# Exponentials of two latent attentions in eight pieces per head, with the negated row maximum as bias and the row sum from the accumulator

## Chip, core and metric

The kernel runs on one core of one Trainium2 chip. The metric is device microseconds of one execution of the whole program, lower is better; the number for a kernel is the median of several executions. The program is a decoder of four layers in eleven stages that follow each other; the change touches two of them.

## What is computed

`x` has 16 sequences of 64 tokens with 256 channels. The two sublayers that the change touches are the third layer's latent cross attention and the fourth (last) layer's latent self attention. Both end in the same softmax over 64 keys, for 16 heads:

```python
# third layer, cross (cut)
q_r = jnp.einsum('bshq,hqr->bhsr', rope(q_big), W_qr)
k_r = jnp.einsum('bld,hdr->bhlr', kv_r, W_kr)
scores = jnp.einsum('bhsr,bhlr->bhsl', q_r, k_r)
attn = jax.nn.softmax(scores, axis=-1)
ctx_c = jnp.einsum('bhsl,bld->bhsd', attn, kv_r)
# last layer, self attention (cut)
scores = jnp.einsum('bqhd,bkhd->bhqk', qf, kf) * (1.0 / np.sqrt(192))
scores = jnp.where(mask, scores, min)      # causal
p = jax.nn.softmax(scores, axis=-1)
o = jnp.einsum('bhqk,bkhd->bqhd', p, v)
```

The second layer's cross attention has the same form, and in the kernel it uses the same function, but the change leaves it as it is.

## The kernel before

All 1024 tokens are kept in SBUF, 128 to a tile, so a tile (`j`, eight of them, `NT`) holds two sequences. `attend` (L549) is the softmax part of all three latent attentions. It writes one program for each engine; the order of instructions on an engine is the order in which they stand there, and semaphores join the engines. It works head by head as a pipeline: a loop over `h` runs on every engine, and in turn `h` the engine does the projection of head `h`, the scores and the softmax of head `g = h - lag` (`lag` is 3 in the two stages here) and the transpose of head `h - lag - 2`.

For one head:

- TensorE writes the scores of the 16 sequences as 128 rows by 8 tiles by 64 keys into PSUM bank 4 or 5 (L569; in the self attention with the causal mask as a first product, L565).
- VectorE takes the maximum over the 64 keys (L684, into `mx`, 128 by 8) and subtracts it from the scores (L688, from PSUM into `pr`, which has three places in SBUF). It counts `centred`.
- ScalarE takes the exponential of all 512 columns in place in one instruction (L652) and counts `expd`.
- VectorE sums (L667), takes the reciprocal (L669) and multiplies (L671). It does this for head `g - 1`, behind the maximum and the subtraction of head `g`.
- TensorE transposes `pr` (L581, `turn`) in a later turn. ScalarE copies the result out of PSUM (L648, into `pT`).
- For every second head TensorE multiplies the two transposed heads by the values (L592, `weigh(u)` for heads `2u` and `2u+1`). ScalarE copies the result out with two instructions for each head of the pair (L633, `copy_context(u, hh)`, in two successive turns). `weigh(u)` waits until both copies of `weigh(u-1)` are made (`ctx`), since there is one pair of PSUM banks for it.
- After the last head TensorE multiplies all contexts by the output weights (L614).

ScalarE's order in a turn is fixed: the context copies (L633), then the copies that belong to the queries, then the copy of the transposed head (L648), then the exponential (L652).

The projections differ. In the cross attention (L1185) TensorE makes them in quarters (`project`, L1134, and `narrow`, L1143), VectorE applies the rotary factors (L1155, L1160, L1164), GpSimd adds (L1183) and ScalarE copies (L1172). In the self attention (L1397) TensorE makes two products of 512 columns for each turn (L1353), VectorE applies the factors (L1378, L1380), ScalarE copies the rows without rotation (L1372) and GpSimd adds the rotated rows (L1393); the scores wait for GpSimd (`q_ready`).

TensorE may write the scores of head `h` over those of head `h - 2` once `centred` says that the subtraction of head `h - 2` has read them.

## Time and profile before

| what | value |
|---|---|
| median of 3 runs | 1553.65 us (1550.98 to 1555.01) |
| the profiled execution | 1560.24 us, its span 1558.3 us |
| TensorE busy | 1361.1 us (87%) |
| VectorE busy | 794.7 us (51%) |
| ScalarE busy | 526.8 us (34%), 959 instructions |
| GpSimd busy | 311.0 us (20%) |
| cross attention's head loop | from 938 to 1123 us of the span |
| self attention's head loop | from 1283 to 1403 us of the span |

The profile is of one execution. Busy time of an engine includes time in which it works beside another; only the wait that ends last in a stretch sets its length. TensorE's matmuls are pipelined and their ends are modelled, so its busy time is read together with the idle time that the profile gives ahead of an instruction. The granted clock is a share of TensorE's full speed: 1.00 is 2.4 GHz and 0.50 is 1.2 GHz.

### The profile page before, as it was taken

The page shows a single profiled execution, that of the slowest core. Times are in us where ns is not written, and L with a number is a line of the kernel's source. Part 1 is how long each engine was busy: PE and PEld are TensorE (multiplying, and loading weights), DVE is VectorE, ACT ScalarE, POOL GpSimd, SP SyncE. Part 2 cuts the span into 40 slices and gives each one's busy share as a digit, 9 for nine tenths or more (in the row PEclk, how much of TensorE's full clock was granted, in tenths as well). Part 3 has the DMA queues.
Part 4 walks back from the last instruction along what each step waited for, and adds up shares of the span by engine and source line. Part 5 has one row for each costly group of instructions (what it writes and reads, how often), then busy time and mean ns, then how long its engine had stood idle before and what let it go on. Part 6 is the DMA issues. An engine that isn't in the chain of part 4 may idle for free. (4 is left out here: it accounts for less than half of the span.)

```text
span 1558.3 us, 27986 instructions
## 1 busy us (share of the span) xinstructions
PE 1361.1 (87%) x11757; PEld 1020.7 (65%) x11757; DVE 794.7 (51%) x1490; ACT 526.8 (34%) x959; POOL 311.0 (20%) x255
## 2 busy tenths in 40 slices
PE   7768997989999988799987989999789569979888
PEld 3348995557877667688846767888675244657555
DVE  5744454553245561433335655878336637852542
ACT  3321223462234562312131331223423323542451
POOL 0143422001102000111100013333002109830100
PEclk9769998899999998899997989999899879989999
DMA  3000002118005000100045070000025300000000
GB/s 104 1 1 4 4 4 76 35 30 177 0 1 183 2 1 1 31 0 1 0 120 164 2 228 0 1 1 1 1 82 191 101 21 1 2 1 28 1 2 27
DMA packets 75036, 63.51 MB, mean 41 GB/s; under 512 B 21016, under 2 KB 72928, under 8 KB 74784
## 3 DMA queue, kind: packets, MB, share of 16 engines
q1 hardware_dynamic: 74144, 59.63, 13.3%
q0 software_dynamic: 768, 2.10, 0.4%
q8 instruction: 93, 1.52, 0.4%
q14 instruction: 31, 0.25, 0.1%
HBM read 53.33 MB, written 8.39 MB: 40 GB/s over the span
## 5 line engine op out<-in xcount | busy, mean ns | idle before, releaser
L1678 PE MATMUL ps<-rounded 128*128 128x512 f32 x384 | 94.0, 401 | 5.8 <-DVE work L1788 5.3
L1134 PE MATMUL ps<-fixed,work 128*128 128x256 f32 x384 | 91.0, 387 | 4.5 <-DVE weights L1160 2.4
L1393 POOL TENSOR_TENSOR work<-weights,work 32x512 f32<-32x512 f32 x64 | 85.6, 1337 | 23.4 <-ACT work L1372 19.7
L1678 PEld LDWEIGHTS ps<-rounded 128*128 128x128 f32 x384 | 72.4, 191 | 25.0 <-issue 6.4
L1183 POOL TENSOR_TENSOR fixed<-fixed,weights 128x768 f32<-128x768 f32 x32 | 57.9, 1809 | 129.0 <-DVE weights L1164 129.0
L1134 PEld LDWEIGHTS ps<-fixed,work 128*128 128x128 f32 x384 | 70.3, 190 | 18.0 <-DVE weights L1160 6.9
L1706 POOL TENSOR_TENSOR rounded<-weights,rounded 128x256 fp32r<-128x256 f32 x32 | 23.5, 754 | 273.3 <-ACT rounded L1712 273.3
L210 PE MATMUL ps<-fixed 128*128 128x128 f32 x160 | 34.2, 338 | 44.1 <-ACT fixed L198 37.8
L633 ACT COPY weights<-ps 64x512 f32<-64x512 f32 x96 | 55.7, 580 | 28.4 <-PE ps L592 26.6
L614 PE MATMUL ps<-work,weights 128*128 128x256 f32 x256 | 59.8, 395 | 5.0 <-ACT weights L633 5.0
L697 DVE TENSOR_TENSOR fixed<-fixed,ps 128x512 f32<-128x512 f32 x12 | 8.2, 688 | 101.3 <-PE ps L614 101.3
L1535 PE MATMUL ps<-weights,work 128*128 128x256 f32 x256 | 59.4, 393 | 0.0
L1602 DVE SCALAR_TENSOR_TENSOR fixed<-ps,work,fixed 128x256 f32<-128x256 f32 x64 | 28.0, 479 | 60.8 <-PE ps L1535 60.8
L614 PEld LDWEIGHTS ps<-work,weights 128*128 128x128 f32 x256 | 50.5, 199 | 12.7 <-ACT weights L633 5.5
L210 PEld LDWEIGHTS ps<-fixed 128*128 128x128 f32 x160 | 19.7, 163 | 56.9 <-ACT fixed L198 24.3
L1788 DVE TENSOR_TENSOR work<-work,ps 128x512 f32<-128x512 f32 x32 | 21.9, 687 | 68.4 <-ACT work L1729 68.4
L1729 ACT ACTIVATE work<-ps 128x512 f32<-128x512 f32 x32 | 19.2, 599 | 111.3 <-PE ps L1678 111.3
L1695 PE MATMUL ps<-weights,work 128*128 128x256 f32 x256 | 56.4, 379 | 0.0
L1535 PEld LDWEIGHTS ps<-weights,work 128*128 128x128 f32 x256 | 50.6, 198 | 8.2 <-issue 0.7
L1172 ACT COPY weights<-ps 128x256 f32<-128x256 f32 x32 | 11.9, 373 | 129.4 <-PE ps L1143 129.4
L198 ACT ACTIVATE fixed<-fixed 128x256 f32<-128x256 f32 x96 | 51.9, 592 | 8.1 <-DVE fixed L181 8.0
L684 DVE TENSOR_REDUCE weights<-ps 128x8 f32<-128x512 f32 x48 | 33.2, 692 | 40.2 <-PE ps L569 39.5
(439 smaller groups left out, 3087.5 us busy)
## 6 DMA issues: line engine op xcount, KB each, us to landing
weights<-in_L_ffn_masksT SPq DMA_DIRECT2D x32, 256.0 KB, 6.2
weights<-in_L_ffn_fc_w SPq DMA_DIRECT2D x16, 256.0 KB
weights<-in_L_xattn_Wq SPq DMA_DIRECT2D x2, 2048.0 KB, 10.1
weights<-in_L_xattn_WoT SPq DMA_DIRECT2D x2, 2048.0 KB, 10.1
sorted_in<-work SPq DMA_DIRECT2D x1, 3072.0 KB, 11.8
work<-sorted_in SPq DMA_DIRECT2D x12, 256.0 KB, 2.9
sorted_out<-work SPq DMA_DIRECT2D x12, 256.0 KB, 2.1
weights<-in_L_ffn_Wg SPq DMA_DIRECT2D x8, 256.0 KB, 4.7
```

What stands on the lines that cost most here:

```text
L198: nc.scalar.activation(to, of, ACT.Identity, bias=k.nshift[:, j:j + 1], scale=k.nrstd[:, j:j + 1]).then_inc(s["n_normed"], 1)
L210: last = nc.tensor.transpose(k.ps[:, banks[i % 2], (2 * c + jj) * P:(2 * c + jj + 1) * P], k.h[:, 2 * i + jj, c * P:(c + 1) * P], k.ident)
L614: last = nc.tensor.matmul(ps[:, (0, 1, 4, 5)[j // 2], (j % 2) * D:(j % 2 + 1) * D], t.ctxT[:, u, j * P:(j + 1) * P], t.pm[:, u, :], start= ...
L633: nc.scalar.copy(dst, src).then_inc(s["ctx"], 1)
L684: nc.vector.tensor_reduce(mx, sc, AX.X, ALU.max).then_inc(s["maxed"], 1)
L1134: last = nc.tensor.matmul(seen[:, a, :], qf[:, c, u, a, :], k.hT[:, c, part * D:(part + 1) * D], start=c == 0, stop=c == KC - 1)
L1183: nc.gpsimd.tensor_tensor(ro[:, v % 2, :, :], ro[:, v % 2, :, :], sn, ALU.add).then_inc(s["roped"], 1)
L1393: last = nc.gpsimd.tensor_tensor(qb[64 + 32 * half:96 + 32 * half, 2 * (u % 2) + e, tok], cs[made, v % 2, :], sn[made, v % 2, :], ALU.add)
L1535: last = nc.tensor.matmul(ps[:, 4 + i, jj * D:(jj + 1) * D], act1[:, (e - 1) % 2, c, j * P:(j + 1) * P], w.fc2[:, e - 1, c, :], start=c == ...
L1602: nc.vector.scalar_tensor_tensor(x[:, j, :], accumulate_bank(j // 2)[:, j % 2, :], comb[:, j, e:e + 1], x[:, j, :], ALU.mult, ALU.add).the ...
L1678: last = nc.tensor.matmul(ps[:, 2 * (n % 2) + i, :], a[:, q % 2, i, c, :], b[:, c, half * BANK:(half + 1) * BANK], start=c == 0 and part = ...
L1695: last = nc.tensor.matmul(ps[:, 4 + i, jj * D:(jj + 1) * D], mid[:, (e - 1) % 2, c, j * P:(j + 1) * P], w.d[:, TURN[e - 1], c, :], start=c ...
```

## The change

`attend` gets an argument `summed`, which is set for the two stages. With it:

- VectorE no longer subtracts. It multiplies the maxima (128 by 8) by minus the scale of the scores, in place, and counts `centred` for that.
- ScalarE reads the scores in PSUM itself, with eight activations of 64 columns for each head, one for each tile: exponential of scale times score plus the negated maximum (a bias of one value for each partition), written into `pr`, with the sum of the 64 columns as accumulator output into `sm`. The last of the eight counts `expd`.
- VectorE no longer sums.
- The wait until `pr` is free again (`turned`, for heads from 3 on) moves from VectorE to ScalarE.
- TensorE waits for `expd` where it waited for `centred`, since the bank is now read until the exponential.

```diff
-def attend(k, block, s, t, key_rows, q_of, q_hooks, scale, causal=None, turn_banks=(2, 3), turned=True, lag=2):
+def attend(k, block, s, t, key_rows, q_of, q_hooks, scale, causal=None, turn_banks=(2, 3), turned=True, lag=2, summed=False):
...
-                pe.wait_ge(s["centred"], h - 1)
+                pe.wait_ge(s["expd" if summed else "centred"], h - 1)
...
-        pe.wait_ge(s["centred"], NH)
+        pe.wait_ge(s["expd" if summed else "centred"], NH)
...
-                nc.scalar.activation(t.pr[:, g % 3, :, :], t.pr[:, g % 3, :, :], ACT.Exp, scale=scale).then_inc(s["expd"], 1)
+                if summed:
+                    if g >= 3:
+                        act.wait_ge(s["turned"], g - 2)
+                    for j in range(NT):
+                        ins = nc.scalar.activation(t.pr[:, g % 3, j, :], ps[:, 4 + g % 2, j * SEQ:(j + 1) * SEQ], ACT.Exp, scale=scale,
+                                                   bias=t.mx[:, g % 2, j:j + 1], accum_out=t.sm[:, g % 2, j:j + 1])
+                    ins.then_inc(s["expd"], 1)
...
-            nc.vector.tensor_reduce(sm, pr, AX.X, ALU.add).then_inc(s["summed"], 1)
-            dve.wait_ge(s["summed"], g + 1)
+            if not summed:
+                nc.vector.tensor_reduce(sm, pr, AX.X, ALU.add).then_inc(s["summed"], 1)
+                dve.wait_ge(s["summed"], g + 1)
...
-            if g >= 3:
-                dve.wait_ge(s["turned"], g - 2)
-            nc.vector.tensor_tensor(pr, sc, bc(mx, 2, SEQ), ALU.subtract).then_inc(s["centred"], 1)
+            if summed:
+                nc.vector.tensor_scalar(mx, mx, -scale, None, ALU.mult).then_inc(s["centred"], 1)
+            else:
+                if g >= 3:
+                    dve.wait_ge(s["turned"], g - 2)
+                nc.vector.tensor_tensor(pr, sc, bc(mx, 2, SEQ), ALU.subtract).then_inc(s["centred"], 1)
```

ScalarE, the last three heads of the self attention, before: the row with L652 is the exponential, the two others are the context copies (L633) and the copy of the transposed head (L648).

```order
L652 ACTIVATE weights<-weights 128x512
L633 COPY weights<-ps 64x4x128 x2
L648 COPY fixed<-ps 128x512
L652 ACTIVATE weights<-weights 128x512
L633 COPY weights<-ps 64x4x128 x2
L648 COPY fixed<-ps 128x512
L652 ACTIVATE weights<-weights 128x512
```

The same place of the changed kernel, where the exponentials are line 656:

```order
L656 ACTIVATE weights<-ps,weights 128x64 x8
L633 COPY weights<-ps 64x4x128 x2
L648 COPY fixed<-ps 128x512
L656 ACTIVATE weights<-ps,weights 128x64 x8
L633 COPY weights<-ps 64x4x128 x2
L648 COPY fixed<-ps 128x512
L656 ACTIVATE weights<-ps,weights 128x64 x8
```

No instruction changed its place; the exponential became eight that read PSUM, between the same neighbours.

VectorE, the last two heads of the self attention, before (L684 maximum, L688 subtraction, L667 sum, L669 reciprocal, L671 multiplication, of which the last three belong to the head before):

```order
L684 TENSOR_REDUCE weights<-ps 128x8
L688 TENSOR_TENSOR weights<-ps,weights 128x512
L667 TENSOR_REDUCE weights<-weights 128x8
L669 RECIPROCAL weights<-weights 128x8
L671 TENSOR_TENSOR weights<-weights 128x512
L667 TENSOR_REDUCE weights<-weights 128x8
L669 RECIPROCAL weights<-weights 128x8
L671 TENSOR_TENSOR weights<-weights 128x512
```

And of the changed kernel, with the maximum at line 693, the negation at 696, the reciprocal at 678 and the multiplication at 680:

```order
L693 TENSOR_REDUCE weights<-ps 128x8
L696 TENSOR_SCALAR weights<-weights 128x8
L678 RECIPROCAL weights<-weights 128x8
L680 TENSOR_TENSOR weights<-weights 128x512
L678 RECIPROCAL weights<-weights 128x8
L680 TENSOR_TENSOR weights<-weights 128x512
```

The subtraction over 512 columns became an instruction of 8 columns, and the sum is gone.

## Rows read from the trace of the kernel before

**Rows 1.** Windows: stretch, length, busy (count) of PE, PEld, DVE, ACT, POOL, clock, DMA.

```profile
1040.00:1060.00 20.00, 19.99 (x156) 16.99 (x155) 16.91 (x26) 6.04 (x12) 6.46 (x4) 1.00 0.00 1
...
1340.00:1350.00 10.00, 10.00 (x92) 6.49 (x89) 9.37 (x16) 5.43 (x10) 8.40 (x8) 1.00 0.01 2
```

**Rows 2.** Timeline, cross loop: start us, duration us, engine, instruction, [idle before, releaser].

```profile
1007.82 0.96 DVE L1155 TENSOR_TENSOR fixed<-ps,weights 128x768 f32<-128x768 f32 x1 [1.03 <-PE ps L1134]
...
1009.12 0.37 ACT L1172 COPY weights<-ps 128x256 f32<-128x256 f32 x1 [4.79 <-PE ps L1143]
```

**Rows 3.** Timeline of the self attention's loop, one turn.

```profile
1331.27 0.59 ACT L648 COPY fixed<-ps 128x512 f32<-128x512 f32 x1
...
1331.75 0.63 ACT L652 ACTIVATE weights<-weights 128x512 f32<-128x512 f32 x1
...
1332.41 1.19 ACT L633 COPY weights<-ps 64x512 f32<-64x512 f32 x2
...
1335.66 1.95 PE L592 MATMUL ps<-fixed,work 128*128 128x128 f32 x16
```

**Rows 4.** Timeline of ScalarE, its other accumulator activations and two back-to-back activations.

```profile
1256.06 0.20 ACT L1270 ACTIVATION_READ_ACCUMULATOR work<-ps 128x1 f32 x1
1256.28 0.22 ACT L1272 ACTIVATE work<-ps 128x64 f32<-128x64 f32 x1
1256.40 0.20 ACT L1272 ACTIVATION_READ_ACCUMULATOR work<-ps 128x1 f32 x1
...
1134.59 1.09 ACT L198 ACTIVATE fixed<-fixed 128x256 f32<-128x256 f32 x2 [0.43 <-DVE fixed L181]
```

**Rows 5.** Groups by line: instruction, count | busy us, mean ns | idle before.

```profile
L1565 ACT ACTIVATE work<-ps,weights 128x512 f32<-128x512 f32 x32 | 22.0, 689 | 67.1 <-PE ps L1508 67.1
L1729 ACT ACTIVATE work<-ps 128x512 f32<-128x512 f32 x32 | 19.2, 599 | 111.3 <-PE ps L1678 111.3
...
L688 DVE TENSOR_TENSOR weights<-ps,weights 128x512 f32<-128x512 f32 x16 | 11.1, 692 | 0.5
...
L667 DVE TENSOR_REDUCE weights<-weights 128x8 f32<-128x512 f32 x16 | 10.8, 676 | 0.0
L669 DVE RECIPROCAL weights<-weights 128x8 f32<-128x8 f32 x16 | 3.3, 203 | 0.6
```

**Rows 6.** Timeline of the cross attention's tail.

```profile
1100.38 0.59 ACT L648 COPY weights<-ps 128x512 f32<-128x512 f32 x1 [1.29 <-PE ps L581]
...
1103.33 3.54 PE L592 MATMUL ps<-weights,work 128*128 128x128 f32 x16
...
1108.57 0.59 ACT L648 COPY weights<-ps 128x512 f32<-128x512 f32 x1 [0.48 <-PE ps L581]
...
1109.44 0.63 ACT L652 ACTIVATE weights<-weights 128x512 f32<-128x512 f32 x1 [0.28 <-DVE weights L688]
...
1111.02 1.11 PE L581 MATMUL ps<-fixed,weights 128*128 128x128 f32 x4 [2.48 <-DVE weights L671]
...
1111.92 3.62 PE L592 MATMUL ps<-weights,work 128*128 128x128 f32 x16
```

**Rows 7.** Timeline of the self attention's tail.

```profile
1380.79 0.58 PE L565 MATMUL ps<-fixed 128*128 128x512 bf16 x1 [3.70 <-POOL work L1393]
...
1389.23 0.59 ACT L648 COPY fixed<-ps 128x512 f32<-128x512 f32 x1 [0.70 <-PE ps L581]
...
1391.68 0.66 PE L581 MATMUL ps<-fixed,weights 128*128 128x128 f32 x4 [2.49 <-DVE weights L671]
...
1392.18 1.95 PE L592 MATMUL ps<-fixed,work 128*128 128x128 f32 x16
...
1395.98 1.18 ACT L633 COPY weights<-ps 64x512 f32<-64x512 f32 x2
...
1397.31 3.48 PE L592 MATMUL ps<-fixed,work 128*128 128x128 f32 x16 [2.75 <-ACT weights L633]
```

**Rows 8.** A window of TensorE alone, cross tail: busy (count), clock, DMA.

```profile
1112.00:1116.00 4.00, 4.00 (x21) 0.50 0.00 0
```

More of the change, by code:

```diff
@@ L651, in _ @@
                 act.wait_ge(s["centred"], g + 1)
-                nc.scalar.activation(t.pr[:, g % 3, :, :], t.pr[:, g % 3, :, :], ACT.Exp, scale=scale).then_inc(s["expd"], 1)
+                if summed:
[6 more added lines that the diff above has]
+                else:
+                    nc.scalar.activation(t.pr[:, g % 3, :, :], t.pr[:, g % 3, :, :], ACT.Exp, scale=scale).then_inc(s["expd"], 1)
         for i in range(NT // 2):
@@ L685, in _ @@
             dve.wait_ge(s["maxed"], g + 1)
-            if g >= 3:
-                dve.wait_ge(s["turned"], g - 2)
-            nc.vector.tensor_tensor(pr, sc, bc(mx, 2, SEQ), ALU.subtract).then_inc(s["centred"], 1)
+            if summed:
+                nc.vector.tensor_scalar(mx, mx, -scale, None, ALU.mult).then_inc(s["centred"], 1)
+            else:
+                if g >= 3:
+                    dve.wait_ge(s["turned"], g - 2)
+                nc.vector.tensor_tensor(pr, sc, bc(mx, 2, SEQ), ALU.subtract).then_inc(s["centred"], 1)
             if h < NH:
@@ L1190, in stage_L2_xattn @@
                 "pe_last": lambda pe: narrow(pe, 2 * NH - 1), "act_last": lambda act: copy_q(act, 2 * NH - 1)},
-               1.0, turn_banks=(3, 3), lag=3)
+               1.0, turn_banks=(3, 3), lag=3, summed=True)
 def load_L3_attn(k, w, sem):
@@ L1398, in stage_L3_attn @@
                {"pe": rotated_rows, "pe_b": other_rows, "act": none, "act_b": act_q, "dve": dve_q,
-                "ready": lambda h: 2 * (h // 2) + 2}, 192 ** -0.5, causal=k.causal, turned=False, lag=3)
+                "ready": lambda h: 2 * (h // 2) + 2}, 192 ** -0.5, causal=k.causal, turned=False, lag=3, summed=True)
 class First:
```

## The prediction

> **What bounds the kernel now.** I read first the windows over the two head loops, to see which engine has no idle time, then the timeline inside one turn, then the timeline of the two tails (the turns after the last projection), and at the end the rows that price an activation with an accumulator.
>
> In both loops TensorE is busy without a break at clock 1.00 [rows 1]. The reader is to see that VectorE, which the change relieves, has more than 3 us of idle time in 20 in the cross loop, and that ScalarE, which it loads, has 14 in the cross loop and 4.6 in 10 in the self attention. In the cross loop VectorE waits for TensorE ahead of its rotary product (1.03 us), not the other way round, and ScalarE waits 4.79 us ahead of a copy [rows 2]. So VectorE's time in the loops is worth nothing as long as TensorE is full.
>
> In the tails there are no projections left, and one head's chain sets the time: maximum, subtraction, exponential, sum, reciprocal, multiplication, transpose, copy, product with the values, two context copies. There the rows show TensorE waiting for L671 twice, 2.48 us in the cross tail and 2.49 in the self tail [rows 6, 7].
>
> **The change, part by part.** All durations are from the one profiled execution (1560.24 us, span 1558.3), which lies 0.4% above the median of 1553.65; I add the differences to the median.
>
> *VectorE.* Each head loses a subtraction of 692 ns and a sum of 676 ns and gains an instruction on 128 by 8, for which the reciprocal of the same size is the nearest row: 203 ns [rows 5]. That is 1.17 us for each of 32 heads, 37 us of VectorE's time. In the loops it lies under TensorE's work: 0. If that cover were gone, at most the whole would count, which no row supports.
>
> *ScalarE, the price of one piece.* The kernel has such an activation already, 64 columns from PSUM with an accumulator output, though without a bias tensor. It shows as two rows: the accumulator is read 0.12 us after the start of the activation, and from the start of a read to the next activation it is 0.22 us, there with a semaphore wait in between [rows 4]. A bias tensor adds 0.09 us (689 against 599 ns, same shape, PSUM to SBUF) [rows 5]. Upper end: 0.12 + 0.22 + 0.09 = 0.43 us for a piece, 3.5 us for a head. In the new code there is no wait between pieces, and two activations of 592 ns without a wait take 1.09 us together, so the second starts 0.1 before the end of the first [rows 4]. If the read overlaps in the same way, a piece is 0.12 + 0.10 + 0.09 = 0.31 us, and a head 2.5. I take the latter and add 0.1 for the last read to come home: 2.6 us, since back-to-back instructions without a wait are what the new code issues. Lower bound: if bias and read cost no issue time, 0.19 for a piece and 1.6 for a head. Before, the exponential held ScalarE for 0.66 us (1331.75 to 1332.41) [rows 3]. So ScalarE gets about 2 us more for each head.
>
> The Trainium skill, page "ScalarE: Activation LUTs", section "What ACT_TABLE_LOAD costs", gives an activation with a bias of one value per partition as 280 ns plus 0.833 ns for each column, and lets back-to-back activations overlap by 93 ns. For 64 columns that is 333 ns alone, of which about 160 lie outside the columns and the bias; eight pieces pay it eight times. By it and the read row, an estimate is 0.34 us for a piece and 2.75 for a head, and the sum below would be about 0.6 us larger. The rows of this trace agree on the 0.09 for the bias and on the overlap.
>
> *Self attention, loop.* ScalarE's order matters: exponential, context copies, then the product `weigh` of TensorE, which waits for both context copies of the pair before. The exponential starts at 1331.75, the copies 0.66 later, and `weigh` runs at 1335.66 [rows 3]. From the start of the copies to the `weigh` that they release it is 1.33 us (1395.98 to 1397.31) [rows 7]. With 2.6 us: 1331.75 + 2.6 + 1.33 = 1335.68. So the slack of 1.9 us is just used up: 0. With 3.5 us it is 0.9 late in each pair of turns, and three such pairs lie ahead of the last GpSimd sum, for which TensorE waits 3.70 us in the tail [rows 7]: up to 2.8 us. The price of a piece decides this term.
>
> *Cross attention, loop.* Here ScalarE has 14 us idle in 20 [rows 1], and its query copy waits 4.79 us for TensorE [rows 2], more than the 2.8 us that even the upper price adds: 0.
>
> *The moved waits.* TensorE's wait for the bank (with its queue of transposes and products behind it) is for the head two before, whose exponential stands two turns earlier on ScalarE; a turn is longer than the 2.8 us that a head gets at most (from L648 to `weigh` alone it is 4.4 us [rows 3]): 0 in the loops and the tails. ScalarE's new wait for `turned` is for a transpose of which it copied the successor just before: 0. Behind it on ScalarE stand the context copies, but it is always satisfied.
>
> *Cross attention, tail.* The exponential of the third last head can start 0.48 after the copy L648 at 1100.38 (the spacing is 1331.27 to 1331.75 [rows 3]), at 1100.86. Then 2.6 and 1.33: `weigh(5)` at 1104.8, before 1103.33, +1.5 [rows 6]. Next, the copy L648 at 1108.57 moves by that. The last exponential follows it by 0.48 instead of 0.87 (it waited 0.28 for the subtraction), a gain of 0.4. Then 2.6 + 1.33 to `weigh(6)`: 1108.57 + 1.5 + 0.48 + 2.6 + 1.33 = 1114.5, before 1111.92 [rows 6]. Sum +2.6. The 2.48 us for L671 go, but what is late next is ScalarE.
>
> *Self attention, tail.* GpSimd's sum holds the second last head until 1380.79, so the earlier exponentials fit in front of it. Then 1389.23 + 0.48 + 2.6 + 1.33 = 1393.6 for `weigh(6)`, before 1392.18: +1.5 [rows 7].
>
> *The clock.* A tail has longer gaps of TensorE now. The same product takes 1.95 us at full clock and 3.5 to 3.6 at the lower one [rows 6, 7], which was granted in parts of the tails [rows 8]. I count one more such product at the lower clock: +1.6, with 0 and 3.2 as ends.
>
> Sum: 0 + 0 + 2.6 + 1.5 + 1.6 = 5.7 us. Forecast 1553.65 + 5.7 = 1559.3 us (+0.37%).
>
> **The rivals.**
>
> *A. Dear pieces.* If the read of the accumulator does not overlap with the next activation, a head costs 3.0 to 3.5 us. For it: the only row of such a pair shows 0.22 [rows 4]. Against it: that row has a wait in it. At 3.5 the cross tail gets twice 0.9 more (+4.4), the self tail +2.4, the self loop +2.8, the clock 1.6 to 3.2: +11 to +13, about 1565.5.
>
> *B. The tails hide more.* The lower clock comes no more often than before, and `weigh(5)` falls on the end of the stretch with the lower clock, and so wins back 0.7 of its 1.5. Then 1.9 + 1.5 = +3.4: 1557.0, within 0.3%. For it: the clock's stretches are short against the tails. If besides that a piece is only 0.2 us, almost nothing is left: 1554.5. Against that: the bias costs 0.09 wherever I see it [rows 5].
>
> *C. Faster: VectorE's chain was the tails' bound and ScalarE keeps up.* The two waits for L671, 2.48 and 2.49 us [rows 6, 7], and the 0.28 for L688 are gone and nothing takes their place: -5.2 us, 1548.4. It decides at the point where ScalarE's eight pieces take less than what VectorE saves plus the old exponential: 0.49 for the subtraction less the negation, 0.68 for the sum, and 0.66, so 1.8 us for a head, or 0.23 for a piece. The lower bound above (0.19) is below it, so it can't be excluded; but then the context copies on ScalarE still stand behind the exponential, which leaves little of it.
>
> *D. The loop of the cross attention is VectorE's after all.* A VectorE with 17 us busy in 20 [rows 1] could be late at a place that the averages hide. But the wait ahead of L1155 is for TensorE [rows 2]. I give nothing to it beyond C.
>
> **How the numbers follow.** Forecast, with the clock's loss: 0.43 (its own range 1558.3 to 1562). A: 0.25. B, both forms: 0.27. C: 0.05, D within it. A kernel in which these tails differ by less than 0.3%, 4.7 us, can't be told from no change. The forecast is 5.7 and reaches from 4.7 to 8; A is slower as a whole; B is the same. So slower 0.66, same 0.29, faster 0.05. The range: below, B's weaker form and some of the spread of the median, 1553.0; above, A's end of +13.5, 1567.0. What is left out is most of C and the very dear pieces.
>
> **What would show each step.** The row of L656 and its accumulator reads: eight and eight, and from the first activation to the context copies 2.6 us. VectorE's L688 and L667 gone, and in the windows of the cross loop a TensorE as full as before. The wait of TensorE ahead of L592 in the self loop near 0 for the forecast, near 0.9 for A. In the tails, TensorE's waits name ScalarE's L633 instead of L671. Wrong would be the prediction if the loops change their period with pieces at 0.31, or if the whole is faster although ScalarE's exponential takes 2.6 us: then VectorE had a part in the bound that I did not see.

## The result and the profile after

The changed kernel takes 1568.36 us (median of 4 runs, 1564.59 to 1570.5) beside 1554.33 us for the kernel before on the same chip (4 runs, 1550.98 to 1555.64): a ratio of 1.0089, 95% interval 1.0067 to 1.0112. The forecast had the sign right, and the size wrong: +14 us where +5.7 was expected, and outside the range (1553.0 to 1567.0).

The page of the changed kernel: its span, and the busy time of each engine with its share and number of instructions.

```profile
span 1562.8 us, 28434 instructions
...
PE 1365.1 (87%) x11757; PEld 1020.8 (65%) x11757; DVE 788.9 (50%) x1458; ACT 583.9 (37%) x1439; POOL 309.3 (20%) x255
```

ScalarE has 480 instructions more and is busy for 57 us more. VectorE, from which two instructions over 512 columns were taken for each of 32 heads, is busy for 5.8 us less. That is the first surprise, and the last section comes back to it.

**The loops.** Windows of the changed kernel in the two head loops (length, then busy time with count of PE, PEld, DVE, ACT, POOL, then clock, DMA), to be held against [rows 1]:

```profile
1040.00:1060.00 20.00, 20.00 (x132) 17.04 (x128) 17.14 (x23) 9.10 (x41) 7.24 (x4) 1.00 0.00 1
1332.00:1342.00 10.00, 10.00 (x79) 6.07 (x79) 6.12 (x11) 7.93 (x31) 7.92 (x7) 1.00 0.01 2
```

TensorE is as full as before and the clock 1.00. From the maximum of head 3 to that of head 13 the cross loop takes 104.36 us and the self loop 60.22 us, in both kernels, to within 0.02 us. Nothing was gained or lost there.

**One head on ScalarE.** Timeline of ScalarE in the self attention (start, duration, engine, line):

```profile
1371.63 0.32 ACT L656 ACTIVATE weights<-ps,weights 128x64 f32<-128x64 f32 x1
1371.84 0.20 ACT L656 ACTIVATION_READ_ACCUMULATOR weights<-ps,weights 128x1 f32 x1
1371.93 0.31 ACT L656 ACTIVATE weights<-ps,weights 128x64 f32<-128x64 f32 x1
...
1373.95 1.20 ACT L633 COPY weights<-ps 64x512 f32<-64x512 f32 x2
```

From one activation to the next it is 0.29 to 0.30 us (1371.63 to 1371.93), and from the first to the context copies 2.32 us; in the other places 2.5. The forecast was 0.31 and 2.6.

**The cross attention's tail**, to be held against [rows 6], where both `weigh` wait for nothing that the row names, since the wait was for the transposes ahead of them:

```profile
1093.57 0.32 ACT L656 ACTIVATE weights<-ps,weights 128x64 f32<-128x64 f32 x1
...
1096.07 1.18 ACT L633 COPY weights<-ps 64x512 f32<-64x512 f32 x2
...
1097.40 3.34 PE L592 MATMUL ps<-weights,work 128*128 128x128 f32 x16 [2.45 <-ACT weights L633]
...
1102.69 0.58 ACT L648 COPY weights<-ps 128x512 f32<-128x512 f32 x1 [0.73 <-PE ps L581]
1103.18 0.32 ACT L656 ACTIVATE weights<-ps,weights 128x64 f32<-128x64 f32 x1
1105.68 1.18 ACT L633 COPY weights<-ps 64x512 f32<-64x512 f32 x2
1107.01 3.75 PE L592 MATMUL ps<-weights,work 128*128 128x128 f32 x16 [2.44 <-ACT weights L633]
```

TensorE's wait ahead of `weigh(5)` and `weigh(6)` now names ScalarE's L633; before, there was none ahead of these two, but 1.41 and 2.48 us for VectorE's L671 ahead of the transposes in front of them, of which 0.17 and 1.25 are left. The chain reads as forecast: copy 1102.69, activations 0.49 later, context copies 2.50 later, `weigh(6)` 1.33 later. From the scores of head 13 (1098.60 before, 1091.32 here) to `weigh(6)` (1111.92 before, 1107.01 here) it is 13.32 before and 15.69 here, so +2.37; to `weigh(5)` (1103.33 and 1097.40) it is 4.73 and 6.08, so +1.35.

**The self attention's tail**, against [rows 7]:

```profile
1377.28 0.38 PE L565 MATMUL ps<-fixed 128*128 128x512 bf16 x1 [3.29 <-POOL work L1405]
...
1384.59 0.58 ACT L648 COPY fixed<-ps 128x512 f32<-128x512 f32 x1
...
1388.90 3.76 PE L592 MATMUL ps<-fixed,work 128*128 128x128 f32 x16 [2.45 <-ACT weights L633]
...
1395.84 3.75 PE L592 MATMUL ps<-fixed,work 128*128 128x128 f32 x16 [2.33 <-ACT weights L633]
```

From the copy of the transposed head to `weigh(6)` it was 2.95 us (1389.23 to 1392.18) and is 4.31 (1384.59 to 1388.90): +1.36. And the product, 1.95 us at full clock before, takes 3.76. But that copy itself comes 1.54 us sooner after the maximum of head 13 than before, since the product ahead of it took 3.19 us at the lower clock before and takes 2.36 here: such a difference mixes the chain with what the clock did just ahead of it.

**Behind the tails.** The stage behind the self attention is a grouped attention that the change does not touch. Windows of TensorE alone over its start (length, PE busy with count, clock, DMA), before:

```profile
1440.00:1450.00 10.00, 7.46 (x68) 1.00 0.14 44
1450.00:1460.00 10.00, 9.44 (x108) 1.00 0.01 2
```

and of the changed kernel:

```profile
1440.00:1450.00 10.00, 8.13 (x50) 0.63 0.00 0
1450.00:1460.00 10.00, 9.78 (x75) 0.69 0.01 2
```

The same eight products of that stage in the timeline, before and of the changed kernel:

```profile
1445.98 1.13 PE L335 MATMUL ps<-work 32*128 32x256 f32 x8
```

```profile
1445.43 2.08 PE L335 MATMUL ps<-work 32*128 32x256 f32 x8
```

The stage's first product and its third exponential (L442), before and of the changed kernel:

```profile
1436.74 1.07 PE L323 MATMUL ps<-fixed 128*32 128x128 f32 x16 [1.73 <-PEq L78]
...
1456.14 1.02 ACT L442 ACTIVATE work<-ps 128x1024 f32<-128x1024 f32 x1 [1.52 <-PE ps L359]
```

```profile
1435.31 1.07 PE L323 MATMUL ps<-fixed 128*32 128x128 f32 x16 [1.73 <-PEq L78]
...
1459.80 1.02 ACT L442 ACTIVATE work<-ps 128x1024 f32<-128x1024 f32 x1 [1.52 <-PE ps L359]
```

From the one to the other it is 19.40 us before and 24.49 after; this stretch is called the start of the grouped attention from here on. So unaltered code pays as much as both tails together. From the start of the third layer's first projection to the end of the span the sum is:

| stretch | before, us | changed kernel |
|---|---|---|
| cross tail (maximum of head 13 to output product) | 23.44 | +3.33 |
| output product of the cross | 30.46 | +1.20 |
| from there to the self attention's first projections (L1353) | 126.5 | -0.3 |
| self tail (likewise) | 26.72 | +1.89 |
| start of the grouped attention | 19.40 | +5.09 |
| all else, both loops among it | 399.1 | +0.6 |
| sum | 625.6 | +11.8 |

The rest of the span, all of it ahead of the stages that the change touches, is shorter in this profile by 7.3 us, though its instructions are the same; so the profiled spans (1558.3 and 1562.8) can't be subtracted to find the price of the change. The same stretch took 932.75 and 926.0 us in two profiles of the kernel before.

From the cross on, TensorE was granted 1.2 GHz for 79.5 us before and for 110.0 in the changed kernel (mean clock 0.94 and 0.91).

### The profile page after: what moved, and what is told of

It reads as the page before. It is cut to its first block and busy times, and to the rows that moved or that the text cites. A ratio compares the mean times of both kernels' runs of the same rounds, so it can differ in the third digit from the quotient of the medians.

```text
span 1562.8 us, 28434 instructions
## 1 busy us (share of the span) xinstructions
PE 1365.1 (87%) x11757; PEld 1020.8 (65%) x11757; DVE 788.9 (50%) x1458; ACT 583.9 (37%) x1439; POOL 309.3 (20%) x255
## 5 line engine op out<-in xcount | busy, mean ns | idle before, releaser
L1405 POOL TENSOR_TENSOR work<-weights,work 32x512 f32<-32x512 f32 x64 | 83.4, 1304 | 25.1 <-ACT work L1384 21.8
L1718 POOL TENSOR_TENSOR rounded<-weights,rounded 128x256 fp32r<-128x256 f32 x32 | 23.5, 755 | 271.6 <-ACT rounded L1724 271.6
L656 ACT ACTIVATE weights<-ps,weights 128x64 f32<-128x64 f32 x256 | 76.4, 332 | 0.1
L633 ACT COPY weights<-ps 64x512 f32<-64x512 f32 x96 | 55.8, 581 | 22.8 <-PE ps L592 21.1
L680 DVE TENSOR_TENSOR weights<-weights 128x512 f32<-128x512 f32 x48 | 60.7, 1264 | 1.6
L187 ACT ACTIVATE fixed<-fixed 128x2 f32<-128x2 f32 x48 | 13.6, 293 | 119.6 <-DVE fixed L171 119.5
L210 PEld LDWEIGHTS ps<-fixed 128*128 128x128 f32 x160 | 20.9, 169 | 57.0 <-ACT fixed L198 24.7
L656 ACT ACTIVATION_READ_ACCUMULATOR weights<-ps,weights 128x1 f32 x256 | 57.8, 226 | 0.0
L1800 DVE TENSOR_TENSOR work<-work,ps 128x512 f32<-128x512 f32 x32 | 21.9, 688 | 68.8 <-ACT work L1741 68.7
```

The lines of the kernel that those rows point to most:

```text
L210: last = nc.tensor.transpose(k.ps[:, banks[i % 2], (2 * c + jj) * P:(2 * c + jj + 1) * P], k.h[:, 2 * i + jj, c * P:(c + 1) * P], k.ident)
L633: nc.scalar.copy(dst, src).then_inc(s["ctx"], 1)
L656: ins = nc.scalar.activation(t.pr[:, g % 3, j, :], ps[:, 4 + g % 2, j * SEQ:(j + 1) * SEQ], ACT.Exp, scale=scale, bias=t.mx[:, g % 2, j:j ...
L680: nc.vector.tensor_tensor(pr, pr, bc(rs, 2, SEQ), ALU.mult).then_inc(s["probs"], 1)
L1405: last = nc.gpsimd.tensor_tensor(qb[64 + 32 * half:96 + 32 * half, 2 * (u % 2) + e, tok], cs[made, v % 2, :], sn[made, v % 2, :], ALU.add)
```

## The experiments

The runs of one group were made on one chip with runs of the kernel before in between. In the diffs `g` is the head, and `hold(k, bank, n)` (L1450) issues `n` products of 128 rows by 512 bf16 columns into a PSUM bank that is not in use; their result isn't used.

### Where the loss sits

**The changed kernel again**, unaltered:

> The changed kernel once more, unaltered. The one profile of it shows 5 to 6 us of loss in the two tails (cross +3.3, self +1.9, the output product +1.2 and back) and 5.1 us in the stage behind the self attention, where nothing was changed but TensorE was granted 1.2 GHz for 13.7 us. Theory T (tails and random clock): the whole is 5 to 8 us slower (ratio 1.003 to 1.005), and in a second profile the stage behind has its former clock. Theory C (the tails shift what follows into the lower clock): 12 to 16 us slower again (1.008 to 1.010), and the stage behind has the lower clock again.

1570.61 us (9 runs), 1.0081 [1.0053, 1.0109]. Its profile from the cross attention's start on: +14.0 us, with cross tail +3.42, self tail +2.00, start of the grouped attention +6.42. The loss repeats, and so does its place, as theory C said; the time at 1.2 GHz is 113.3 us.

**The change in one stage only**, by leaving `summed=True` out of one of the two calls:

```diff
-                "ready": lambda h: 2 * (h // 2) + 2}, 192 ** -0.5, causal=k.causal, turned=False, lag=3, summed=True)
+                "ready": lambda h: 2 * (h // 2) + 2}, 192 ** -0.5, causal=k.causal, turned=False, lag=3)
```

> The change in the third layer's cross attention alone. T: +3 to +4.5 us (1.002 to 1.003). C: the same and no more, if the clock behind the self attention is what costs: then at most 1.004. If the cost lay in the cross stage's loop, it would be over 1.006.

Cross alone: 1561.87 us, 1.0045 [1.0024, 1.0067], a little above what either theory gave it.

> The change in the last self attention alone. T: +2 to +3.5 us (1.001 to 1.002). C: +6 to +9 us (1.004 to 1.006), with the lower clock in the stage behind.

Self attention alone: 1558.49 us, 1.0016 [0.9997, 1.0035]. The two excesses, 0.45% and 0.16%, make 0.61% together; the whole change costs 0.81%. In both profiles the grouped attention starts at full clock (19.40 us), and from the cross on they are +7.2 and +1.6 us. So theory C's 1.004 to 1.006 for the self attention alone did not come true: the lower clock in the stage behind does not follow from the change in the self tail. The 0.2% that are missing to the whole (3 us) lie within what the intervals leave open. The profile of the self attention alone shows one thing more: its cross attention is the old code, and yet its cross tail takes 21.84 us where the kernel before's takes 23.44.

**Loops against tails.** `tail_old` uses the new form for all heads but the last three, `tail_new` for the last three alone:

```diff
+    def fused(g):
+        return summed and g < NH - 3
...
-                if summed:
+                if fused(g):
```

(the other one with `g >= NH - 3`; `fused` stands in place of `summed` at each head's wait, negation and sum too).

> The change in both stages for the first 13 heads, the last three heads in the old form (subtraction, one exponential, sum on VectorE). T and C, which both start from the tails: within 0.2% of before (1.000 +- 0.002), and TensorE's waits in the tails name the multiplication again. If the loops carry the loss, it stays: 1.006 or more.

1553.6 us, 0.9985 [0.9969, 1.0]: without the tails nothing is lost, and perhaps a little gained.

> The new form for the last three heads of both stages alone, the first 13 in the old form; the counterpart of the run with the tails in the old form, which came out at 0.9985. If the loss is in the tails and what they bring, the whole of it is here: 1.006 to 1.010. If it needs the loops' longer ScalarE work as well, half of it or less (1.004).

1565.96 us, 1.0077 [1.0056, 1.0098]: three heads in each of two stages carry the whole loss. Its profile (cross tail +3.98, self tail +2.87, +7.35 in all from the cross on) is of an execution in which the grouped attention ran at full clock, and which is the fastest of its six (1560.35 us, mean clock 0.921; the others 1564.94 to 1568.95 at 0.910 to 0.918). Its median is 10.5 us above that of the kernel before in the same group (1555.46).

### What of the eight pieces costs

The accumulator out, eight activations with a bias left, and VectorE sums again:

```diff
-                                                   bias=t.mx[:, g % 2, j:j + 1], accum_out=t.sm[:, g % 2, j:j + 1])
+                                                   bias=t.mx[:, g % 2, j:j + 1])
...
-            if not summed:
-                nc.vector.tensor_reduce(sm, pr, AX.X, ALU.add).then_inc(s["summed"], 1)
-                dve.wait_ge(s["summed"], g + 1)
+            nc.vector.tensor_reduce(sm, pr, AX.X, ALU.add).then_inc(s["summed"], 1)
+            dve.wait_ge(s["summed"], g + 1)
```

> Eight activations of 64 columns with the maximum as bias, but without accumulator output; VectorE sums as before the change (676 ns). A piece is then 0.31 less the overlap of 0.09, 0.22 us, a head 1.8 instead of 2.3 us on ScalarE. The two tails then lose about 1 us less each than with the change: +3 us in the tails, in all 1.003 to 1.007. If the loss were VectorE's short chain or the moved waits, it would be as large as with the change (1.008).

1562.45 us, 1.0038 [1.0019, 1.0057]: within the forecast, and about half of the loss is gone, which it would not be if VectorE's short chain or the moved waits carried it. Its timeline of ScalarE:

```profile
1374.55 1.76 ACT L656 ACTIVATE weights<-ps,weights 128x64 f32<-128x64 f32 x8
1376.13 1.20 ACT L633 COPY weights<-ps 64x512 f32<-64x512 f32 x2
```

A head takes 1.58 us, 0.198 for a piece; with the accumulator it was 2.32, 0.290 for a piece, so the read takes 0.092 us of ScalarE's time for each piece although its row shows 0.19 to 0.25. The Trainium skill, page "ScalarE: Activation LUTs", section "What ACT_TABLE_LOAD costs", gives 280 ns plus 0.833 for each column for an activation with a bias of one value per partition, and an overlap of 93 ns; an estimate for this piece is 0.24 us without the read, by which the head would be 1.9. In this trace the first activation's row is 0.32 long and it is 0.198 from start to start, so the overlap is larger here, and the measurement decides. The sum on VectorE is back in the chain with 0.68 us, so this form is no gain over the old one either.

### The clock in the tails

`hold` ahead of the changed kernel's last three `weigh` (the expectation speaks of two) and of its output product, in both tails, keeps TensorE at work where it waits for the chain:

```diff
             if h >= lag + 4 and (h - lag) % 2 == 0:
+                if summed and h >= NH + 1:
+                    hold(k, 0, 4)
                 weigh((h - lag - 4) // 2)
+        if summed:
+            hold(k, 0, 5)
```

> The changed kernel; in the two tails TensorE does four products without use of 512 bf16 columns ahead of each of the last two (cross) or last two (self) products with the values, and five ahead of the output product, where it waited 2.3 to 2.5 us for ScalarE. ScalarE's work is the same. Theory C (two thirds of the loss is lower clock, which the tails' gaps bring and which lasts into the output product and the stage behind): the tails get back 2 to 3 us and the stage behind the self attention its 5 us: +3 to +6 us against before, ratio 1.002 to 1.004. Rival S (the whole loss is ScalarE's chain, the clock in the stage behind is of another origin): 1.007 to 1.009 as the changed kernel.

1555.7 us, 1.0007 [0.9993, 1.0021]. Of the changed kernel's excess of 0.81% only 0.07% is left, though nothing of the change was undone and work was added. Its timeline of TensorE in the cross tail:

```profile
1101.46 2.02 PE L592 MATMUL ps<-weights,work 128*128 128x128 f32 x16 [1.59 <-ACT weights L637]
...
1106.88 1.03 PE L1469 MATMUL ps<-fixed 128*128 128x512 bf16 x4
...
1109.70 2.02 PE L592 MATMUL ps<-weights,work 128*128 128x128 f32 x16 [1.79 <-ACT weights L637]
```

The waits for L637 (the copies, L633 before) are still there; the products take 2.02 us and not 3.34 to 3.75. The cross tail is 22.85 us, the changed kernel's 26.77, before's 23.44, and the output product takes 28.77 us where it took 31.66, and 30.46 before. The stage behind did not get its 5 us back, as it was expected to: its start takes 24.17 us in this profile. So the 0.07% is not the old loss removed; the kernel before also pays for the lower clock in its tails and its output products, and this kernel no longer does.

The same treatment for the kernel before, to price the chain alone at equal clock:

```diff
+            if held and h == NH + lag - 2:
+                hold(k, 0, 2)
+            if held and h == NH + lag:
+                hold(k, 0, 5)
...
+                if held and h == NH + lag + 2:
+                    hold(k, 0, 4)
...
+        if held:
+            hold(k, 0, 5)
```

> The kernel before with products without use in TensorE's own waits of the two tails (two, five and four, and five ahead of the output product), 16 in each tail against 17 (cross) or 13 in the run of the changed kernel that came out at 1.0007. At a clock that is full in both, the change costs what ScalarE's chain costs: the hand sum says +2.6 and +1.5 us, 4.1 us. So this kernel should be at 0.997 to 0.998. If the lower clock was the whole of the loss, it is at 1.000 like the changed one; if the kernel before loses as much to the clock as the changed one, 0.993.

1554.55 us, 0.9999 [0.9981, 1.0017]. This is a miss: the cross tail becomes 19.74 us (from 23.44) and the self tail 25.42 (from 26.72), and all the same nothing is won in the median. The start of its grouped attention takes 24.71 us where before's takes 19.40. What was saved in the two tails, 5.0 us, came back there, +5.3, in code that was not touched. The two output products are 1.7 us shorter each, so that its profile is still 3.5 us below before's from the cross on (622.1 and 625.6); that execution is the second fastest of twelve.

The two held kernels make the best pair for the chain. Both run the cross tail at clock 1.00 throughout, and there the changed one takes 3.11 us more (22.85 and 19.74), where the unheld ones differ by 3.33. So the longer cross tail is ScalarE's chain, and not, in the main, the clock: the holds took 3.9 us from the one kernel and 3.7 from the other. In the self tail it is 2.89, of which up to 1.1 is the last `weigh` at the lower clock (3.15 us and 2.02). From the cross on the two profiles differ by 4.7 us, both with a slow grouped attention, at 80.7 and 76.1 us of 1.2 GHz. The forecast had 4.1 for the chain. The medians (1.0007 and 0.9999, intervals that overlap) can't separate that from nothing, and the holds don't stand in quite the same places.

### The stage behind

Does the grouped attention lose time because TensorE has short gaps at its start? Products were put in those gaps, in the changed kernel and in the kernel before:

```diff
+    second, k.seen = hasattr(k, "seen"), True
...
+                if t == 0 and second:
+                    hold(k, 2, 3)
...
+                if t == 0 and second:
+                    hold(k, 2, 2)
```

> The changed kernel; in the stage behind the self attention TensorE does three products without use of 512 bf16 columns where it waited 1.41 us for VectorE, and two where it waited 0.77 for ScalarE, in its first turn only. Of the eight profiles of other kernels that I have beside the changed one, four show 1.2 GHz for 14 to 17 us behind this place (5 to 6 us longer) and four don't, whatever their tails are. If that draw costs the changed kernel more often than before, this gives back 4 to 5 us: 1.004 to 1.006. If the change's tails carry the loss by themselves: 1.008.

1566.6 us, 1.0063 [1.0038, 1.0089], where the unaltered changed kernel had 1.0081 with an interval that overlaps. The profile shows the grouped attention at full clock and 19.40 us, but in this profile the cross tail is +4.64 and its output product +1.34. So the hold does its work where it stands; what it gave back in the median (1.0081 to 1.0063) is less than the 4 to 5 us that it was to bring, and isn't clear of the noise.

> The kernel before with the same products in the first turn of the stage behind the self attention. If the lower clock at that place is a draw that the kernel before meets as well, in about half of its executions: -2 to -3 us, 0.998. If the kernel before never meets it: 1.000.

1556.84 us, 1.001 [0.9994, 1.0027]: nothing to repair there in the kernel before, as expected.

Is it chance in a profile? The kernel before twice more, and the changed kernel once more:

> The kernel before, one profile more. Open is how often it meets the lower clock at the start of the stage behind the self attention (5 to 6 us) and in the cross tail (1.6 us): its one profile has the second, not the first. If the first is a draw that any kernel meets half the time, one of the two new profiles should show it.

> As the look before it: none of two with the lower clock behind speaks for an uneven draw, both with it against one.

> The changed kernel, a third profile. Both earlier ones show the lower clock at the start of the stage behind, 5.1 and 6.4 us. If its tails bring that about, this one shows it too; if it is an even draw, it is as likely not to.

The kernel before takes 625.6, 625.6 and 625.7 us from the cross on in its three profiles: in these three it meets the clock in the same way. That is not so for its code in general: `tail_old`, `self_only`, `before_gqa_hold` and `before_later` have the old code in the last three heads of the cross, and their cross tail is 21.8 to 21.9 us, not 23.4 to 23.5. The changed kernel takes 637.4, 639.6 and 630.4. In the third its grouped attention starts so:

```profile
1440.00:1450.00 10.00, 8.57 (x92) 1.00 0.01 2
1450.00:1460.00 10.00, 9.17 (x98) 1.00 0.01 2
```

full clock, 19.40 us, with the same instructions. Over the tail of the cross and the start of its output product the first and the third profile of the changed kernel differ in the same way, first the one, then the other:

```profile
1100.00:1126.00 26.00, 17.50 (x98) 0.65 0.00 1
```

```profile
1100.00:1126.00 26.00, 17.48 (x111) 0.85 0.00 1
```

The third is +4.8 us against before, with 79.3 us at 1.2 GHz where before has 79.5. So this pair, too, prices the chain at equal clock, 4.8 us, and what the first two have beyond it, 7.0 and 9.2 us, goes with 30.5 and 33.8 us more at 1.2 GHz. The medians fit the first two better: of the nine executions of the changed kernel in `after_again` one is as fast as the third (1557.16 us at a mean clock of 0.923), the other eight take 1564 to 1576 at 0.905 to 0.916.

**The causal test.** If the position of the stage's start decides, then a kernel without any change in the tails must lose the same once the grouped attention starts a little later. The kernel before, with five idle products at that stage's start:

```diff
+    second, k.seen = hasattr(k, "seen"), True
...
+            if second:
+                hold(k, 2, 5)
             ask(0)
```

> The kernel before; in the stage behind the self attention TensorE does five products without use (512 bf16 columns, 0.21 us each at full clock, 1.07 in all) ahead of its first product, so that all that follows in the stage comes 1.1 us later. Nothing else is changed. If it is only where the stage's first waits fall against the instants at which the granted clock can change that decides, the kernel before now meets the lower clock there as well: +6 to +7.5 us, 1.004 to 1.005. If the lower clock comes from the tails of the changed kernel, it is +1.1 us, 1.0007.

1562.3 us, 1.005 [1.0036, 1.0064], or 7.9 us for products that take 1.24: what the first of the two cases gave. The stage starts 1.17 us later and its start then takes 24.15 us in place of 19.40. Its timeline and windows of TensorE:

```profile
1430.49 1.24 PE L1456 MATMUL ps<-fixed 128*128 128x512 bf16 x5 [1.73 <-PEq L78]
...
1441.44 2.08 PE L336 MATMUL ps<-work 32*128 32x256 f32 x8
```

```profile
1430.00:1440.00 10.00, 7.81 (x61) 0.92 0.34 107
1440.00:1450.00 10.00, 9.52 (x46) 0.50 0.00 0
1450.00:1460.00 10.00, 9.64 (x98) 0.89 0.01 2
```

The five products are added work, and the clock falls all the same. So none of the change's instructions is needed for this loss. Over all nineteen profiles of this study the start of the grouped attention takes either 19.40 us (twelve) or 24.15 to 25.82 (seven), never between.

That it is the place against the instants at which the clock can change, and not the added products, is seen over all profiles together. The trace records every change of the granted clock, and in each profile the changes lie on one evenly spaced row of instants. Place the stage's first product against this row: in the nine profiles with 19.40 us and no idle products in the stage, it falls into one band 0.67 us wide; in all seven slow ones, `before_later` among them, it falls outside, by 0.25 us or more. The three profiles with idle products in the stage's gaps have 19.40 us; one of them (`before_gqa_hold`) falls into the band and had nothing to lose, the two others (`after_gqa_hold`, `split_held`) fall outside and keep full clock all the same, so there the products did what they were to do.

### Away from ScalarE

In both tails the last links are the two context copies of a pair on ScalarE. Half of each copy of the last two pairs was given to VectorE, idle there, in the kernel before and in the changed kernel:

```diff
-                copy_context((h - lag - 5) // 2, (h - lag - 5) % 2)
+                u, hh = divmod(h - lag - 5, 2)
+                copy_context(act, nc.scalar.copy, u, hh, (0,) if u >= NH // 2 - 2 else (0, 1))
...
         normalise(dve, NH - 1)
+        for u in (NH // 2 - 2, NH // 2 - 1):
+            for hh in range(2):
+                copy_context(dve, nc.vector.tensor_copy, u, hh, (1,))
```

> The changed kernel, where in the tails of all three latent attentions VectorE copies one half (64 partitions) of the contexts of the last two pairs and ScalarE the other. ScalarE has 1.2 us less ahead of the last two products and behind the last. If ScalarE is what is late in the tails: the self and cross tails gain 1.2 to 2.4 us each against the change, the first latent attention's 1.2 to 2.4 as well: -4 to -7 us against the change, near 1.003 against before. If TensorE's clock alone decides, under 2 us.

The changed kernel with it: 1553.54 us, 0.9987 [0.9974, 1.0]. That is some 15 us under the changed kernel (1.0081), twice what was expected.

> The kernel before with the same halved context copies in the three tails. Each tail has two copies of 0.6 us less ahead of the last product and two less behind it: -2 to -2.4 us a tail, -6 to -8 us in all (0.995 to 0.996), and less lower clock. If the tails were bound by VectorE's chain or TensorE, no change (0.999 to 1.001).

The kernel before with it: 1545.3 us, 0.9933 [0.9914, 0.9953]. The gain, 10.0 us, is again more than the 6 to 8 expected. The last product and the output product in the cross tail, before and then with the halved copies:

```profile
1118.73 2.02 PE L592 MATMUL ps<-weights,work 128*128 128x128 f32 x16 [2.33 <-ACT weights L633]
1123.24 12.10 PE L614 MATMUL ps<-work,weights 128*128 128x256 f32 x47 [2.48 <-ACT weights L633]
```

```profile
1108.60 2.02 PE L592 MATMUL ps<-weights,work 128*128 128x128 f32 x16 [1.37 <-ACT weights L631]
1112.13 8.04 PE L614 MATMUL ps<-work,weights 128*128 128x256 f32 x36 [1.51 <-DVE weights L631]
```

The waits were 2.33 and 2.48 us and are 1.37 and 1.51. The edit frees ScalarE in either kernel, and between the two the old softmax is the faster by 8 us (0.9933 against 0.9987, intervals apart). In their profiles the two tails differ by 6.7 us (25.44 and 25.70 against 21.54 and 22.94), and both have a slow grouped attention (24.72 and 25.69); how much of it is chain and how much clock isn't separated.

Last, the halved copies with `hold` in the tails and at the grouped attention's start (as above):

```diff
+            if h == NH + lag:
+                hold(k, 0, 4)
...
+                if h == NH + lag + 2:
+                    hold(k, 0, 2)
                 weigh((h - lag - 4) // 2)
+        hold(k, 0, 3)
         pe.wait_ge(s["ctx"], 2 * NH)
```

> The kernel before with halved context copies on ScalarE and VectorE (0.9933 alone), and products without use in TensorE's waits of the three tails (four, two and three) and in the first turn of the stage behind. If the clock still takes what its profile shows (a tail product at 1.2 GHz, 1.6 us, in each tail, and 6 us behind): 0.988 to 0.991. If the products delay what waits for them, 0.994 or more.

1532.11 us, **0.9855 [0.9832, 0.9877]**: 1.4% below the kernel before, and faster than both kernels; it was expected at 0.988 to 0.991. Its cross tail (TensorE, ScalarE and VectorE):

```profile
1098.21 1.95 PE L597 MATMUL ps<-weights,work 128*128 128x128 f32 x16
1100.19 0.58 ACT L641 COPY weights<-ps 64x512 f32<-64x512 f32 x1 [1.20 <-PE ps L597]
1100.19 1.42 DVE L641 COPY weights<-ps 64x512 f32<-64x512 f32 x2 [0.98 <-PE ps L597]
```

`weigh` takes 1.95 us, the first copies start together on both engines, the cross tail is 17.45 us (23.44 before), the self tail 22.81 (26.72), the start of the grouped attention 19.40, and from the cross on it is 611.3 us (625.6). The new softmax was not run with both edits.

## Why the prediction was wrong, point by point

| step of the forecast | forecast | measured |
|---|---|---|
| a piece on ScalarE | 0.31 us | 0.29 |
| a head, first activation to copies | 2.6 us | 2.32 to 2.50 |
| both loops | 0 | 0.02 at most |
| moved waits | 0 | 0 (no period changed) |
| `weigh(5)`, cross | +1.5 | +1.35 |
| `weigh(6)`, cross | +2.6 | +2.37 (the whole tail +3.11 at full clock) |
| `weigh(6)`, self | +1.5 | +1.36 (the whole tail +1.89, +2.89 with holds) |
| VectorE for each head | -1.17 us | +0.19 in the cross, -0.54 in the self attention, hidden |
| both chains together | +4.1 | +4.7 and +4.8, in two pairs of profiles |
| the clock | +1.6, ends 0 and 3.2 | +7.0, +9.2 and about 0, in three profiles |
| sum, on the median | +5.7 | +14 |

- **What bounds the kernel, and what becomes the bound: right.** TensorE in the loops, ScalarE's chain in the tails. `tail_old` and `tail_new` show that only the last three heads count.
- **ScalarE's piece: right**, and the choice between the bounds too: the read overlaps. Rival A, dear pieces, came nearest to the measured time (1565.5) but by a mechanism that isn't there; a head is at the cheap end. One figure of the estimate beside it is wrong: of the 333 ns, less 53 for the columns and 93 for the bias, 187 are left and not about 160; nothing in the sum rests on it.
- **The self loop: right.** The slack was just enough.
- **The negation: wrong, without a consequence.** Priced at 203 ns by the reciprocal, it took 1.06 us on average in the cross loop, five times that, beside GpSimd; the cover held.
- **The clock: this step failed.** The term was sized as one more product at the lower clock, inside the tails, +1.6 with 3.2 as the upper end. Of the +11.8 us of the profiled execution, the two tails have 5.2, near what the chain costs at equal clock (4.7 and 4.8). The other 6.6 are in stages that the change doesn't touch: 5.09 at the start of the grouped attention, 1.20 in the output product, and small ones of both signs. In the second profile it is 8.6 of 14.0. The prediction treated everything behind a tail as moved along unchanged. It is moved, but against instants of the clock that don't move with it.
- **A half-step of the same error:** the differences were put on the median of before as if each execution met the clock in the same way. The three profiles of the kernel before agree (625.6, 625.6, 625.7), but its cross tail is 1.6 us shorter in four profiles of kernels with the same code for these heads, and the changed kernel has 630.4 to 639.6. In the favourable execution the forecast is off by 0.9 us, and that is in part luck: the clock's 1.6 us are not in it, and the chain is 0.7 dearer than its term.
- **Rival B**, no more clock loss, held in one of three profiles (79.3 us at 1.2 GHz against 79.5), and there the change costs 4.8 us, not 3.4. In the two others it is 110.0 and 113.3 us, and the medians go with them. **C** is refuted by the sign, and by ScalarE's L633 as the releaser in the tails. **D** supposed a relief of VectorE in the cross loop that did not come about (its busy time rose); what speaks against it is TensorE's 20.00 busy us of 20.
- **The range** had A's end as +13.5 where A's own sum ends at +13; the measured time lies above both.
- **Open:** how the chain's price divides between the two tails, since one low stretch of the clock more or less moves a tail by 1 to 2 us; what sets where a program's stages fall against the instants of the clock in an execution, and so how often each kernel draws the slow case; and how large the gain of `hold` in the changed kernel's grouped attention is, which the intervals don't separate from zero.

## What to carry to other kernels

Cutting an instruction into eight pieces makes a price for each piece on an engine that may look idle; what decides is the place where that engine is last in the chain, here three heads of sixteen. Read a wait on TensorE in a tail twice, once for its length and once for what clock the work behind it gets, also in stages that the edit leaves alone: a stage with short gaps can change by 5 us when its start moves by 1, so look at several executions of both kernels. A few idle products in the waits can hold the clock, but they move what follows as well: alone they gave the kernel before nothing (0.9999), together with halved copies and products in the next stage's gaps they took part in the 1.4%. And where a tail ends in copies on one engine, halve them between two.

## What the runs showed of the hardware

**A shift of 1.2 us cost 8.** `before_later` above: five products of 1.24 us at the start of a stage, and the whole program is slower by 7.9 us (1.005 [1.0036, 1.0064]), of which the profile shows 1.17 for the shift, 4.75 for the stage's start at the lower of the two clock levels and 0.8 behind it. The idle products that keep the clock in the tails move this stage too: `before_hold` gained 5.0 in the tails and lost 5.3 there.

**VectorE gains little when GpSimd works beside it.** Timelines of VectorE and GpSimd in the changed kernel's cross loop:

```profile
1062.43 1.23 DVE L696 TENSOR_SCALAR weights<-weights 128x8 f32<-128x8 f32 x1
...
1066.88 2.24 DVE L680 TENSOR_TENSOR weights<-weights 128x512 f32<-128x512 f32 x1
```

```profile
1061.82 1.81 POOL L1195 TENSOR_TENSOR fixed<-fixed,weights 128x768 f32<-128x768 f32 x1 [3.19 <-DVE weights L1176]
...
1066.76 1.81 POOL L1195 TENSOR_TENSOR fixed<-fixed,weights 128x768 f32<-128x768 f32 x1 [3.12 <-DVE weights L1176]
```

The negation of 128 by 8 ends at 1063.66, GpSimd's addition at 1063.63; in the tail, without GpSimd, it takes 0.17 us. The multiplication takes 2.24 and ends 0.55 behind GpSimd's addition; in the tail it takes 0.69. Windows of VectorE alone over the cross and the self attention, each from its first products to its output product (length, busy with count, clock, DMA), before:

```profile
932.75:1123.24 190.49, 133.59 (x208) 0.97 0.01 3
1271.20:1403.27 132.07, 88.87 (x140) 0.94 0.00 1
```

and of the changed kernel:

```profile
925.46:1119.28 193.82, 136.57 (x192) 0.96 0.01 4
1268.13:1402.07 133.94, 80.21 (x124) 0.91 0.00 1
```

In the cross attention's 16 heads the subtractions (11.1 us) and the sums (10.9) went, the negations brought 16.1, and the multiplications grew from 20.9 to 29.6: VectorE is busy for 3.0 us more. In the self attention it is busy for 8.7 us less. The Trainium skill, page "SBUF — State Buffer", section "SBUF: two separate sides", says that a VectorE instruction with two SBUF inputs and a GpSimd instruction that reads SBUF take a shared pair of ports for the whole instruction, and that the other one is blocked until then. The trace agrees for the multiplication, whose two inputs lie in SBUF, and the negation ends with GpSimd's addition in the same way; the subtraction and the maximum, which read PSUM, and the sum with its one SBUF input kept their 0.68 to 0.69 us. None of it reached the end of the span, since VectorE was hidden, but as a forecast of VectorE's relief the 37 us were wrong by a factor of six: the page of the profile shows 5.8.
